# The head of a decoder-layer kernel, reordered: TensorE work on constants, x loaded by halves, the first softmax's chain ahead of weight splits, later loads moved behind the first toeplitz rows

## The reference, cut to what matters

```python
def attn(x):       # x: layernorm of the input
    z = softmax(einsum('bse,he->bsh', x, W_A) * 0.25, axis=1)   # over the 512 positions
    roll[b,h,i,j] = z[b,h,(i-j) % 512] if j <= i else 0          # a toeplitz matrix per head
    v = einsum('bse,fe->bsf', x, W_V).reshape(B, S, 16, 16)
    return einsum('bhij,bjhd->bihd', roll, v).reshape(B, S, E) @ W_O.T + b_O
def xattn(c, x):   # causal, one head of 256, keys and values from the context c
    return softmax_causal((x @ WQ) @ (c @ WK).T / 16) @ (c @ WV)
def ffn(x):        # 2 shared experts (128 wide), 16 routed (64 wide), top 2 of 16
    h = silu(x @ wg) * (x @ wu);  return sum over experts of comb * h @ wd
x = x + attn(ln(x));  x = x + xattn(ctx, ln(x));  x = x + ffn(ln(x))
```

## Time and profile before

| what | value |
|---|---|
| median of 3 runs | 593.81 us (592.59 to 594.73) |
| the profiled execution | 591.93 us, of which the span from first to last instruction is 590.1 us |
| PE busy | 551.2 us (93%) |
| DVE busy | 442.2 us (75%) |
| ACT, POOL busy | 235.7 us (40%), 180.0 us (30%) |
| mean granted TensorE clock | 1.000 |

### The profile page before, as it was taken

The page is one execution under the profiler, slowest core; times in us unless marked ns, Lnnn a source line. Parts: engine busy times, 40 slices in busy tenths (PEclk is TensorE's granted clock), DMA queues, the critical chain, the costliest instruction groups (busy, mean ns, idle before and its releaser), DMA issues. The chain is left out here.

```text
span 590.1 us, 13620 instructions
## 1 busy us (share of the span) xinstructions
PE 551.2 (93%) x5116; PEld 373.3 (63%) x5116; DVE 442.2 (75%) x1132; ACT 235.7 (40%) x463; POOL 180.0 (30%) x221
## 2 busy tenths in 40 slices
PE   2798899899999999999999999999999999999897
PEld 1576567566685667766686667666766676666455
DVE  5777687768886698868886898769876777677644
ACT  3574545444344333343244333343343323333232
POOL 2323150322522144122522342224421342132123
PEclk9999999999999999999999999999999999999999
DMA  8895695892449913594439742893169225300431
GB/s 274 298 335 181 201 372 181 164 350 97 108 82 253 315 55 88 113 291 140 108 84 257 232 107 59 183 332 89 55 136 307 88 80 118 69 2 0 111 71 36
DMA packets 90704, 94.74 MB, mean 161 GB/s; under 512 B 28192, under 2 KB 76192, under 8 KB 90400
## 3 DMA queue, kind: packets, MB, share of 16 engines
q1 hardware_dynamic: 90656, 94.09, 56.8%
HBM read 75.66 MB, written 12.12 MB: 149 GB/s over the span
## 5 line engine op out<-in xcount | busy, mean ns | idle before, releaser
L631 POOL TENSOR_TENSOR mid<-gated,mid 128x512 f16<-128x512 f32 x72 | 86.5, 1202 | 246.9 <-ACT mid L783 246.8
L783 ACT ACTIVATE mid<-gated 128x512 f16<-128x512 f32 x72 | 45.1, 626 | 105.6 <-DVEq L1090 105.6
L144 PE MATMUL wide<-w_d,mid 128*128 128x256 f16 x288 | 78.5, 273 | 0.1
L146 PE MATMUL wide<-w_d,mid 128*128 128x256 f16 x288 | 78.5, 272 | 0.0
L145 PE MATMUL wide<-w_d,mid 128*128 128x256 f16 x288 | 78.5, 272 | 0.0
L1071 DVE SCALAR_TENSOR_TENSOR gated<-gated,score 128x512 f32<-128x512 f32 x72 | 49.0, 681 | 37.1 <-ACT gated L778 35.9
L144 PE MATMUL score<-h3T,w_gu 128*128 128x512 f16 x160 | 60.7, 379 | 1.6 <-DVEq L124 1.5
L145 PE MATMUL score<-h3T,w_gu 128*128 128x512 f16 x160 | 60.6, 379 | 0.0
L146 PE MATMUL score<-h3T,w_gu 128*128 128x512 f16 x160 | 60.6, 379 | 0.0
L144 PE MATMUL rows<-h3T,w_gu 128*128 128x512 f16 x160 | 60.6, 379 | 0.0
L145 PE MATMUL rows<-h3T,w_gu 128*128 128x512 f16 x160 | 60.6, 379 | 0.0
(11 more groups left out here) (216 smaller groups left out, 1358.5 us busy)
## 6 DMA issues: line engine op xcount, KB each, us to landing
toep<-z_scratch SPq DMA_DIRECT2D x14, 2048.0 KB, 18.1
stage<-comb_scratch SPq DMA_DIRECT2D x32, 512.0 KB, 7.9
x_in<-in_xr SPq DMA_DIRECT2D x8, 512.0 KB, 11.2
toep<-z_scratch SPq DMA_DIRECT2D x4, 1024.0 KB, 9.9
x_bo<-in_x SPq DMA_DIRECT2D x8, 512.0 KB, 12.0
qT<-q_scratch SPq DMA_DIRECT2D x7, 512.0 KB, 3.8
vx<-v_scratch SPq DMA_DIRECT2D x7, 512.0 KB, 5.3
out<-x_out SPq DMA_DIRECT2D x7, 512.0 KB, 3.0
```

The source lines that it names most:

```text
L144: pe.matmul(out, stationary[0], moving[0], start=start, stop=False, **kw)
L146: return pe.matmul(out, stationary[1], moving[0], start=False, stop=stop, **kw)
L631: pool.tensor_tensor(mid_slot(j, 1, late), gate_slot(j, late), mid_slot(j, 0, late), ALU.subtract).then_inc(mid_split.sem, 1)
L783: act.activation(mid_slot(j, 0, late), gate_slot(j, late), ACT.Copy).then_inc(mid_hi.sem, 1)
```

## The change

It touches only the prologue and the iterations 0 and 1.
- PE: 48 matmuls on two constant tiles (`ident16` by `future`, 128 columns, into `wide`) stand ahead of the first transposes. The transposes of batch 0 come in row blocks (`turn_halves`), two blocks on each half of x.
- x of batch 0 is loaded in two transfers of 256 KB; statistics, reciprocal deviation and normalising run by halves.
- ACT and DVE split `wq` and `wk` behind the first `h1T`, and `wvx` and `wo` behind the first softmax's chain. ACT splits context 0's columns ahead of that chain.
- `gu_r` is loaded in two halves of 1 MB: the first directly behind the store of z, ahead of the four toeplitz transfers; the second once heads 0 to 7 have landed, together with context 2, which now stands ahead of the residual x.
- In iteration 1 the last two quarters of `gu_r` are split behind the copies of the toeplitz result, and ACT splits context 2's columns behind `mixT`.

```diff
+WARM = 48
...
+                if first:
+                    sp.dma_start(x_in[:, 0:2], rows_of[:, 0:2]).then_inc(half_x[0], 16)
+                some = slice(2, C) if first else slice(0, C)
+                sp.dma_start(x_in[:, some], rows_of[:, some]).then_inc(x_loaded.sem, 16)
...
+            def load_gates(k):
+                n = names.index("gu_r")
+                sp.dma_start(staged["gu_r"][:, k], loads[n][1].rearrange("(k p) n -> p k n", p=P)[:, k]).then_inc(
+                    gu_r_loaded if k else w_loaded[n], 16)
...
                 if name == "gu_r":
                     load_x(1, -1)
+                    continue
...
                                  z_parts[:]).then_inc(z_stored.sem, 16)
+                    if not m:
+                        load_gates(0)
...
+                if f and not m:
+
+                    sp.wait_ge(first_toep_loaded, 32)
+                    load_gates(1)
+                    load_context(2)
                 if f and not d:
                     load_residual(it)
                 if f and not m:
-                    load_context(2)
                     load_context(3)
...
-            reciprocal_deviation(0, 0)
+            for half in range(2):
+                some = slice(2 * half, 2 * half + 2)
...
@@ scalar
-                    part_weights(range(MIDDLE, len(pieces) - LATE_PIECES))
+                    part_weights(range(MIDDLE, len(pieces) - LATE_PIECES - 2))
...
                 if first:
-                    part_context_columns(2)
+                    part_weights(range(len(pieces) - LATE_PIECES - 2, len(pieces) - LATE_PIECES))
                 if f:
                     part_values(it, it, 0)
                 if first:
                     part_context(1, (2,))
                     part_turned(it, it - 1, mixT, mixT_hi, "mix")
+                    part_context_columns(2)
...
-            part_weights(range(EARLY))
+            part_weights(range(2))
             part_turned(-1, 0, h1T, h1T_hi, "h1")
-            part_weights(range(EARLY, MIDDLE))
+            part_weights(range(2, EARLY))
+            part_context_columns(0)
             z_powers(0)
             part_z(0)
             part_product()
-            part_context_columns(0)
+            part_weights(range(EARLY, MIDDLE))
...
@@ vector
-            x_statistics(0)
+            for half in range(2):
+                loaded, stats_sem, aggr = half_x[0:3] if not half else (x_loaded.sem, stats_done[0].sem, aggr_done[0].sem)
...
             part_weights(range(2))
-            normalise(0, -1, 0, x_in, x_in)
-            part_weights(range(2, EARLY))
             part_turned(-1, 0, h1T, h1T_hi, "h1")
             turned.reach(dve, turned.taken, -1)
-            part_weights(range(EARLY, MIDDLE))
+            rows.take(dve, 0, "v0")
+            part_weights(range(2, EARLY))
             z_max(0)
             z_invert(0)
             part_z(0)
             part_product()
+            part_weights(range(EARLY, MIDDLE))
...
@@ tensor
-            pe.wait_ge(h_ready[0].sem, h_ready[0].at(0, 2))
-            turn(-1, "h1", x_in)
+
+            pe.wait_ge(const_made, 9)
+            for n in range(WARM):
+                pe.matmul(wide[:, 0, 0:P], ident16[:], future[:], start=True, stop=True, skip_group_check=True)
+            turn_halves(-1, "h1", x_in, h_ready[0], 0)
```

More of the change, by code:

```diff
@@ L348, in decoder_layer @@
         h2_normed = sig("h2_normed", 1)
+        half_x = [sem(f"half_x_{name}") for name in ("loaded", "stats", "aggr", "eps", "rstd")]
         x_biased = sig("x_biased", 1)
@@ L448, in load_x @@
                     sp.wait_ge(h1p_split.sem, h1p_split.at(b - 4, 1))
-                sp.dma_start(x_in[:], xr[b].rearrange("(c p) e -> p c e", p=P)).then_inc(x_loaded.sem, 16)
+                rows_of = xr[b].rearrange("(c p) e -> p c e", p=P)
+                first = isinstance(b, int) and b == 0
+                if first:
+                    sp.dma_start(x_in[:, 0:2], rows_of[:, 0:2]).then_inc(half_x[0], 16)
+                some = slice(2, C) if first else slice(0, C)
+                sp.dma_start(x_in[:, some], rows_of[:, some]).then_inc(x_loaded.sem, 16)
             def load_residual(b):
@@ L681, in iteration @@
                         reciprocal_deviation(it - 1, 2, 1)
-            reciprocal_deviation(0, 0)
+            for half in range(2):
+                some = slice(2 * half, 2 * half + 2)
+                aggr, eps, rstd_sem = half_x[2:] if not half else (aggr_done[0].sem, eps_added[0].sem, rstd_done[0].sem)
+                pool.wait_ge(aggr, 1)
+                pool.sem_inc(held[pool.engine], 1)
+                pool.tensor_scalar(var_eps[0][:, some], mean_var[0][:, some, 1], EPS, X_H ** -2, ALU.add,
+                                   ALU.mult).then_inc(eps, 1)
+                pool.wait_ge(eps, 1)
+                pool.tensor_tensor(rstd[0][:, some], var_eps[0][:, some], minus_half[:, some],
+                                   ALU.pow).then_inc(rstd_sem, 1)
             iterations(pool, iteration, finish, 0)
@@ L694, in part_weights @@
                     name, _, dst, _, _ = loads[n]
-                    act.wait_ge(w_loaded[n], 16)
+                    act.wait_ge(gu_r_loaded if name == "gu_r" and k.start == 1 else w_loaded[n], 16)
                     act.activation(dst[:, 0, k, at], staged[name][:, k, at], ACT.Copy, scale=X_W).then_inc(w_hi, 1)
@@ L1343, in iteration @@
                     add_y(it - 2)
-            x_statistics(0)
+            for half in range(2):
+                loaded, stats_sem, aggr = half_x[0:3] if not half else (x_loaded.sem, stats_done[0].sem, aggr_done[0].sem)
+                dve.wait_ge(loaded, 16)
+                statistics(0, x_in, range(2 * half, 2 * half + 2)).then_inc(stats_sem, 1)
+                dve.wait_ge(stats_sem, 1)
+                dve.sem_inc(held[dve.engine], 1)
+                for c in range(2 * half, 2 * half + 2):
+                    last = dve.bn_aggr(mean_var[0][:, c], stats[0][:, c])
+                last.then_inc(aggr, 1)
+            for half in range(2):
+                dve.wait_ge(rstd_done[0].sem if half else half_x[4], 1)
+                for c in range(2 * half, 2 * half + 2):
+                    last = dve.tensor_scalar(x_in[:, c], x_in[:, c], mean_var[0][:, c, 0:1], rstd[0][:, c:c + 1],
+                                             ALU.subtract, ALU.mult)
+                last.then_inc(h_ready[0].sem, 1)
             part_weights(range(2))
-            normalise(0, -1, 0, x_in, x_in)
-            part_weights(range(2, EARLY))
             part_turned(-1, 0, h1T, h1T_hi, "h1")
             turned.reach(dve, turned.taken, -1)
-            part_weights(range(EARLY, MIDDLE))
+            rows.take(dve, 0, "v0")
+            part_weights(range(2, EARLY))
             z_max(0)
```

1 line of the change is left out of this document (added).

## The result

The changed kernel takes 589.62 us (588.32 to 591.26, 8 runs), the kernel before 592.89 us (592.57 to 594.73, 8 runs) beside it: a ratio of 0.9936, with a 95% interval of 0.9922 to 0.9950. It is 3.3 us faster; I had forecast 590.9 and a gain of 2.9, from 593.81. The profiled execution took 590.94 us, with a span of 589.0 us, which is only 1.1 us less than the 590.1 of before.

A forecast was written before the change was run, and what follows sets the result against it. The middle is bound by TensorE; the head by PE's waits and slow clock. Toeplitz(1) 3.4 us earlier less 0.7 in iteration 1, 2.7 to 3.1 left, taken as 2.9: 593.81 becomes 590.9 us, range 589.2 to 593.2.

The forecast's parts named there:

- the place: All edits fall in the first 100 us; the first 48 us get shorter, the TensorE-bound middle is untouched.
- the first chain: First softmax, from x to z's store: z_parts done 2.85 us earlier, at 16.3; bounds 1.3 and 3.3.
- the sign: The whole kernel gets faster: 0.72, with 0.19 for same.
- So 3.4 - 0.7 = 2.7 us is left at projection: Iteration 1: toeplitz(1) 3.4 us earlier, less 0.5 to 1.0 us more before output projection, leaves 2.7 us.
- moves along: Behind first output projection: later loads, contexts and batch 2's x keep the same gaps, so its gain carries to the end.
- My chain: Iteration 1, toeplitz(1) to projection: two gate quarters ahead of the first value, 0.5 to 1.0 us more.
- the z product itself then takes 1.49 us in place of 2.66: Head, six matmuls on PE: the high clock level after the constants' matmuls saves 1.2 us.
- hidden under it: Head: DVE's splits of wq and wk, done about 12.3, lie under the z product, which ends at 12.6.
- 2 x 0.68: Head: two weight splits on DVE at 0.68 us each.
- the transfers: Toeplitz transfers: the last lands about 35.0 instead of 38.2, bounds 33 and 37; toeplitz(1) starts 3.4 us earlier.
- -0.8 + 1.0 - 0.5: Last toeplitz landing: 2 MB gone from ahead, 1 MB of gu_r between, less residual x; beside the chain's 2.85.
- The rival "slower": The 1 MB ahead of the toeplitz transfers delays the last landing to 41.1 at worst: 596 us; chance 0.08.

The follow-up runs named there:

- before_again: The kernel before, unchanged, run again for a second profile: 594.36 us, span 592.6 us.
- nowarm: The changed kernel without the 48 matmuls on constants: 591.87 us, 0.9966 of the kernel before.
- head_only: The changed kernel's new prologue alone, with transfers, gate quarters and context 2's columns as in the kernel before: 594.21 us, 1.0014 of the kernel before.
- tail_only: The kernel before with only the moved transfers, late gate quarters and context 2's columns, old prologue: 594.40 us, 1.0007 of the kernel before.
- again: The changed kernel unaltered, run a second time as a control: 590.62 us, 0.9961 of the kernel before.
- again2: The changed kernel unaltered, control in the series with moved gate quarters: 588.86 us, 0.9926 of the kernel before.
- quarter: The changed kernel with 0.5 MB of gu_r's first half ahead of the store of z, the other 0.5 MB behind: 590.16 us, 0.9951 of before.
- between: The changed kernel with both late gate quarters split between ACT's two copies of the toeplitz result: 589.72 us, 0.9932 of the kernel before.
- one_between: The changed kernel with one of the two late gate quarters split between ACT's two copies: 590.37 us, 0.9934 of the kernel before.
- gate0_early: The changed kernel with gu_r's first half (1 MB) issued ahead of the store of z, behind batch 1's x: 592.69 us, 0.9986 of the kernel before.
- late2: The changed kernel with the last two gate quarters behind the second value and z's maximum: 596.50 us, 1.0057 of the kernel before.
- fill: The changed kernel with 30 more matmuls on constants between the transposes and the z product: 591.25 us, 0.9967 of the kernel before.
- quarter_fill2: The quarter kernel with 12 matmuls on constants between the two toeplitz products: 589.20 us, 0.9931 of the kernel before.
- one_between_fill2: The one_between kernel with 20 matmuls on constants between the two toeplitz products: 588.72 us, 0.9917 of the kernel before.
- fill2: The changed kernel with 20 matmuls on constants between the two toeplitz products: 589.62 us, 0.9938 of the kernel before.
- before_fill2: The kernel before with 22 matmuls on constants between the two toeplitz products: 595.71 us, 1.0041 of the kernel before.

## Why the prediction's time came near, and which of its steps were wrong

**Right: the place, the first chain and the sign.** Normalising ended at 7.83 (forecast 8.1), h1T at 10.68 (11.1), z was stored at 16.96 (16.3), context 0 came at 18.85 behind DVE's split of w_o, as said (18.3), the second transposes at 26.54 (26.2), toeplitz(0) at 31.61 (31.3), the last landing at 35.4 (35.0), toeplitz(1) at 35.51 (34.9). Normalising of batch 1 met POOL again, 3.04 us.

**Wrong: "So 3.4 - 0.7 = 2.7 us is left at projection", and that what follows "moves along".** This is the step that failed, and the time came near 590.9 by luck. In the pair of profiles that the sum was made for, 0.33 us was left at projection; over the two profiles of before and the three of the change it is 1.4 in the mean. From toeplitz(1) to projection it is 11.32 us against 8.90 in that pair, a loss of 2.4 where I had 0.7. Of this 1.33 lies behind the second copy: DVE's two splits (0.8), and 0.5 where POOL had begun beside the second of them. The other 1.09 lies in the toeplitz product: 0.94 us of it is PE's stop, which no term of mine held. But before_again loses as much there by its clock (6.37 us from toeplitz(1) to the transposes, the change 6.24), so that this part is no price of the change; the first profile of before was short for its kernel. My chain had DVE's splits right and left out that the 4.9 us of idle time ahead of them are of little use: the splits stand behind the copy that ends it, and their weights land only at 38.8.

**What followed did not move along.** The spans 589.0, 588.8 and 587.1 against 590.1 and 592.6 give six differences between 1.1 and 5.5 us, 3.05 in the mean, near the medians' 3.3. With 1.4 at projection, 1.6 us was won behind it, where my forecast had nothing. By nowarm and head_only it goes with the 48 matmuls and not with the new order: between the first and the last projection, before, before_again, tail_only and nowarm, which don't have them, take 446.0 to 446.7 us, and the change, again, again2, head_only, quarter and between, which do, 443.7 to 444.1. It is no rule: one_between, gate0_early and late2, with the same matmuls, take 444.8, 445.5 and 451.7, and fill, with 30 more, 446.0. Of the 2.3 us that the change wins there over before, 1.3 lie between 104 and 244 us, where before has two slow DMA transposes of mixT and the change none (last section). So the forecast of 2.9 came near 3.3 by errors that cancel: in the mean some 0.5 us too much up to toeplitz(1) and 0.7 in iteration 1, and 1.6 further back that I had not counted. The time was also reckoned from 593.81, where the runs of before had 592.89 in the end.

**Wrong in size: "the z product itself then takes 1.49 us in place of 2.66".** The 48 matmuls did raise the clock for the transposes (1.04 to 1.30 us in the change, 2.08 in nowarm). But PE then idled 1.95 us for h1T, and the z product ran its last three to five matmuls at the 1.2 GHz level in all three profiles of the change (2.1 to 2.5 us). fill shows that the term was worth little anyway: with the product fast, "hidden under it" no longer holds for the splits of w_q and w_k, which took 2.25 us for the two beside POOL's columns of context 0 (at 11.48), not 2 x 0.68. I had put POOL's work next to DVE's without charging for it. Of the 1.2 us forecast for the product 0.16 came in; 0.3 us was made up by its earlier start, and z_parts was 0.6 us late.

**Right in sum, unclear in its parts: the transfers.** I gave 0.8 us for the 2 MB no longer ahead of the store, and -0.8 + 1.0 - 0.5 for the last landing beside the chain's 2.85. From the store's issue to toeplitz(1) it is 19.13 us in both profiles of before and 18.41 to 18.55 in the change: 0.6 to 0.7 us gained where I had 0.3. The store alone is no steady witness. From its issue to the first toeplitz transfer it is 3.0 to 3.1 us in the kernel before, 1.6 to 3.0 in the change, up to 3.8 in its variants with no gate weights ahead of the store, 3.7 and 4.15 with 0.5 MB, 4.65 with 1 MB and 7.57 with the 2 MB. So the gain was conditional: with the prologue moved alone, the store stays behind the bulk. I treated prologue and transfers as two terms to be added; head_only (1.0014) and tail_only (1.0007) show that neither is one. The rival "slower" had the other end of it, the 1 MB ahead of the toeplitz transfers, and tail_only is its case with an unmoved store: no loss and no gain. The Trainium skill (DMA: Bandwidth & Descriptors, "Queues, rings and completion order") says that each DMA engine consumes its ring's descriptors in order. The landings agree: 22.1 and 22.2 us for gate weights and store before, 24.4 and 24.6 in head_only, 20.8 and 21.0 in gate0_early.

## What to carry to other kernels

Look at what stands ahead of a small store in the queue at the moment that it will be issued *after* the change: moving a chain earlier gains nothing while its store lands behind bulk traffic, and then load order and compute order only pay together. Work that is deferred is on the path when it stands behind the event that ends its engine's idle time, and it can't be put into that time before its data have landed. And a gain below 1% is not to be read from one pair of profiles: the spans of one kernel differed by 1.9 us (three profiles) and 2.5 us (two). In these profiles 48 added matmuls went with 1 to 2 us won or lost at places that the change doesn't touch: leave added instructions out by themselves and look at the whole trace, as nowarm does.

## What the runs showed of the hardware that I had not expected

**Packets of 16 KB with instructions, and where they fall matters.** They run over a DMA queue of their own, which doesn't name the engine; where its packets are recorded, one comes for every 250 or so of PE's instructions. A stretch of small matmuls, like a toeplitz product, often has a stop of PE: 0.66 to 1.10 us in the change, again, again2, fill, late2, quarter_fill2, one_between and one_between_fill2, 0.41 in fill2, and in before_fill2 0.78 just ahead of toeplitz(1) and 1.32 behind it. Each of these eleven ends 2.3 to 2.6 us after the start of such a packet; that is why I read them as waits for instructions, and nothing else shows it. (The profile also calls 2.41 us ahead of toeplitz(0) in head_only "issue", but that wait ends as a toeplitz transfer lands, at 34.0.) Of the other profiles all but the first of before have the clock at one half in toeplitz(1) instead, at about the same cost: none of the 18 but that one gets from toeplitz(1) to the transposes in less than 5.7 us. Adding matmuls shifts the later packets: near toeplitz(1) they start at 31.6, 38.0 and 44.1 us in nowarm, at 36.4 and 43.8 in the change. One that falls into the DMA transpose of mixT goes with a longer landing; the change from 489.5 to 491.5 us:

```profile
q1 hardware_dynamic: 961, 0.25, 156.8%
q8 instruction: 1, 0.02, 3.8%
...
mixT<-mix SPq DMA_TRANSPOSE x1, 4.6
```

The waits for mixT there, 480 to 500 us, in the change and before:

```profile
  PE rows L145: 1.6, 1
...
DMA to landing us min/median/max: 3.1/3.8/4.6
```

```profile
  PEld rows L144: 0.2, 1
...
DMA to landing us min/median/max: 3.1/3.1/3.2
```

Before, the same thing happens at 101 us (4.6 us, and PE waits 1.11 us at 105.47), where the change has 0.26 us for another reason, and at 169 and 238 us (4.2 and 4.8 us), where the change has 3.1. The 18 profiles hold 252 of these transposes. With a packet starting up to 3 us behind their issue, 37 of 56 landed after more than 3.3 us, up to 4.9, and all 21 of those with the packet 0.77 to 2.4 us behind; without one, 1 of 196 did. I didn't try to place packets by themselves, so the coincidence is shown and its cause is argued.

**The clock falls again soon after it rose, or not.** Behind the 48 matmuls and the transposes, 1.95 us of idle time was followed by the fall in the change's three profiles and in head_only, late2, between, fill2 and quarter_fill2, and not in gate0_early, quarter, one_between and one_between_fill2. The two groups differ earlier: in the first the block of 48 took 5.03 to 5.28 us, in the second 4.34 to 4.46, so the clock had risen sooner there. The kernels are the same up to there, so it differs by execution. At toeplitz(1), behind 1.4 us of waiting and with very small matmuls, it fell in before_again and not in before, at a price of 1.2 us.
